# Attention and pair products on one core: six instead of four of a tile's eight score pieces are kept, and x lives in a ring of chunk slots

## The reference, cut to what matters

```
# layer 0, on n = group_norm(x)
f, g, h = Wq n + bq, Wk n + bk, Wv n + bv        # 32, 32 and 256 channels
s       = f^T g                                   # 4096 x 4096 for each batch
beta    = softmax(s, over the first index)
x       = x + gamma * (h @ beta)
# layer 1, on n = group_norm(x)
y       = relu(bn(w1 n + b1))                     # 32 channels
packed  = all 528 products y[i] * y[j]
x       = x + relu(bn(w2 packed + b2))
```

## Time and profile before

| | us |
|---|---|
| median of 3 runs | 2135.08 (2133.08 to 2136.22) |
| the profiled execution | 2135.18 |
| its span | 2133.4 |
| TensorE busy | 2081.3 |
| VectorE busy | 1623.2 |
| ScalarE busy | 1608.0 |
| GpSimd busy | 1321.3 |

### The profile page before, as it was taken

One profiled execution on the slowest core, in us unless ns is written; L12 is line 12 of the kernel. 1 busy time (PEld: TensorE's weight loads), 2 busy tenths in 40 slices (PEclk: granted clock), 3 DMA queues, 4 the chain that ended last, 5 costly groups with the idle time before them and its releaser, 6 DMA issues.

```text
span 2133.4 us, 48577 instructions
## 1 busy us (share of the span) xinstructions
PE 2081.3 (98%) x17838; PEld 1640.4 (77%) x17838; DVE 1623.2 (76%) x3491; ACT 1608.0 (75%) x2582; POOL 1321.3 (62%) x1984
## 2 busy tenths in 40 slices
PE   4899999999999999999999999999999999999999
PEld 2688888888878877877878777777887778777854
DVE  7687877778877777877778887776876767777767
ACT  4577877777777777878777787777877777777767
POOL 3254455556566676776657677676756656566656
PEclk9999999999999999999999999999999999999999
DMA  6054555455467776667378576776635555464622
GB/s 204 21 81 75 75 88 83 84 84 82 81 119 141 138 135 143 135 118 139 71 149 152 117 142 119 142 143 126 130 59 114 117 103 113 97 122 76 118 66 80
DMA packets 592493, 233.63 MB, mean 110 GB/s; under 512 B 541024, under 2 KB 547936, under 8 KB 592224
## 3 DMA queue, kind: packets, MB, share of 16 engines
q1 hardware_dynamic: 592256, 230.53, 56.4%
HBM read 71.83 MB, written 19.92 MB: 43 GB/s over the span
## 4 chain that ended last, share of the span: by engine, by line
PE 92%; DVE 2%; ACT 2%; issue 1%; DMA 1%; SPq 1%; POOL 0%; DVEq 0%; ACTq 0%
PE acc L1763 21%; PE acc L1751 20%; PE acc L1752 20%; PE sps L1576 5%; PE tps L1556 5%; PE acc L1556 5%; PE tps L1627 4%; PE acc L1550 3%; PE tps L1629 2%; PE acc L1627 1%; PE tps L1591 1%; PE tps L1537 1%; PE tps L1613 1%; PE acc L1629 1%; ACT xh L1276 1%
## 5 line engine op out<-in xcount | busy, mean ns | idle before, releaser
L1136 POOL TENSOR_TENSOR kb<-ks,kb 128x512 f16<-128x512 f32 x504 | 599.3, 1194 | 409.6 <-DVE kb L860 235.9
L1314 ACT ACTIVATE ph<-sps,esc 128x512 f16<-128x512 f32 x520 | 356.7, 686 | 345.8 <-PE sps L1576 336.4
L1751 PE MATMUL acc<-hth,ph 128*128 128x257 f16 x2080 | 484.5, 273 | 0.0
L1752 PE MATMUL acc<-htl,ph 128*128 128x256 f16 x2080 | 484.1, 273 | 0.0
L1751 PE MATMUL acc<-hth,kt 128*128 128x257 f16 x2016 | 469.9, 273 | 0.0
L1752 PE MATMUL acc<-htl,kt 128*128 128x256 f16 x2016 | 469.4, 273 | 0.0
L1326 ACT ACTIVATE ks<-ks,kbias,esc 128x512 f32<-128x512 f32 x504 | 407.0, 808 | 0.0
L865 DVE TENSOR_TENSOR pl<-sps,ph 128x512 f16<-128x512 f32 x520 | 355.2, 683 | 48.2 <-ACT sps L1315 46.7
L1315 ACT ACTIVATE sps<-sps,esc 128x512 f32<-128x512 f32 x520 | 340.5, 655 | 0.0
L1763 PE MATMUL acc<-hth,pl 128*128 128x257 f16 x2080 | 318.3, 274 | 0.0
L1763 PE MATMUL acc<-hth,kt 128*128 128x257 f16 x2016 | 308.8, 274 | 0.0
(11 more groups left out here) (253 smaller groups left out, 3606.3 us busy)
## 6 DMA issues: line engine op xcount, KB each, us to landing
rt<-turned SPq DMA_DIRECT2D x96, 256.0 KB, 5.0
xt<-x SPq DMA_DIRECT2D x36, 512.0 KB, 4.3
xb<-x SPq DMA_DIRECT2D x32, 512.0 KB, 5.5
out<-zt SPq DMA_DIRECT2D x45, 256.0 KB, 2.8
kt<-kb SPq DMA_TRANSPOSE x504, 3.2
yb<-turned SPq DMA_DIRECT2D x36, 128.0 KB, 2.8
rt<-turned SPq DMA_DIRECT2D x72, 64.0 KB, 2.3
turned<-yb SPq DMA_DIRECT2D x12, 256.0 KB, 2.1
```

The source lines that it names most:

```text
L1136: tt(kb[:, m % KB_RING, 1], ks[:, m % KS_RING], kb[:, m % KB_RING, 0], ALU.subtract).then_inc(kl_ok, 1)
L1314: A(ph[:, v % SLOTS], sps[v % 2][:], ACT.Exp, scale=esc[:]).then_inc(ph_ok, 1)
L1751: mm(bank[:, 0:C + 1], high[:, q], hth[:, c * QT + q], start=(s8 == 0 and q == 0), stop=False)
L1752: mm(bank[:, 0:C], high[:, q], htl[:, c * QT + q], start=False, stop=False)
```

## The change

Steps 1, 2, 3, 5, 6 and 7 of a tile are kept; only 0 and 4 are scored a second time. The rings get 9, 4 and 5 places, and the kept pieces' work gets positions written out for each of the six. To have room, x becomes a ring of 14 chunk slots (`XR`; before it was 16 chunks), `xn` a single chunk buffer that is handed over by halves, and the order of the value chunks changes. Chunks that are not in the ring when they are needed go through `xt`: 46 passes instead of 36. The statistics of batches 2 and 3 are taken in batch 0 (`LATER_STATS`), each into its own `bx`.

```diff
-KEPT_STEPS = (1, 3, 5, 7)
+KEPT_STEPS = (1, 2, 3, 5, 6, 7)
+EXP_AT = (1, 4, 5, 6, 7, 8)
+CAST_AT = (None, 3, None, 5, 6, 7)
+LOW_AT = (2, 3, 4, 6, 7, 8)
+TURN_AT = (3, 4, 6, 7, 8, 10)
+DIVIDE_AT = 4
+ROW_AT = 6
-KS_RING = 6
-KB_RING = 3
-KT_RING = 4
+KS_RING = 9
+KB_RING = 4
+KT_RING = 5
+XR = 14
-        xb = [sb(f"xb{i}", [P, H2, HW], f32) for i in range(2)]
+        xb = sb("xb", [P, XR, H2, CH], f32)
-        xn = sb("xn", [P, 2, H2, CH], f32)
+        xn = sb("xn", [P, H2, CH], f32)
-        VORD = (6, 0, 1, 2, 3, 4, 5, 7)
+        VORD = (4, 0, 5, 1, 6, 2, 3, 7)
+        def x_slot(b, c):
+            return (b * NCH + c) % XR
+        NEXT_STATS = tuple((J, t) for J, ts in ((0, (8, 11, 15)), (1, (11, 15, 21)), (2, (11, 18))) for t in ts)
+        LATER_STATS = ((3, 2), (3, 13), (3, 20), (4, 2), (4, 9), (4, 17), (4, 25), (5, 2), (5, 9), (6, 18), (6, 21), (6, 25),
+                       (7, 2), (7, 6), (7, 10), (7, 14))
+        def in_place(b, c):
+            return b == 0 or (c < XR - NCH if b == 1 else c < 4)
+        LOAD_AT = [0] + [USED[use] + 2 for use in THROUGH[:-1]]
...
-            for c in range(NCH):
+            for c in range(XR - NCH):
                 load(1, c)
...
-                        if t % NCH in (2, 4, 6) and is_kept_tile(tile + 1):
-                            turn(tile + 1, t % NCH // 2 - 1)
-                        if t % NCH == 1 and is_kept_tile(tile):
-                            turn(tile, KEPT - 1)
+                        while passed < len(THROUGH) and LOAD_AT[passed] <= (b * NCH + J) * NT + t:
+                            pass_through(*THROUGH[passed])
+                            passed += 1
+                        for r in range(KEPT):
+                            if t % NCH == TURN_AT[r] % NCH and is_kept_tile(tile + 1 - TURN_AT[r] // NCH):
+                                turn(tile + 1 - TURN_AT[r] // NCH, r)
...
-                if k >= 2:
-                    dve.wait_ge(xl_ok, k - 1)
-                for h in range(1 if job in SHARED_OUT else H2):
+                for h in range(halves_of(job)):
+                    if k:
+                        dve.wait_ge(xl_ok, H2 * (k - 1) + h + 1)
...
-                        if s8 in (3, 7) and is_kept_tile(tile + 1):
-                            kept_high(tile + 1, s8 // 2)
+                        if s8 in CAST_AT and is_kept_tile(tile + 1):
+                            kept_high(tile + 1, CAST_AT.index(s8))
```

More of the change, by code:

```diff
@@ L100, in build @@
         ot = sb("ot", [P, QT, C], f32)
-        bst = [sb(f"bst{i}", [P, H2, NCH, 6], f32) for i in range(2)]
+        bst = sb("bst", [P, H2, NCH, 6], f32)
+        bx = [sb(f"bx{i}", [P, H2, NCH, 6], f32) for i in range(B)]
         bag = [sb(f"bag{i}", [P, H2, 2], f32) for i in range(2)]
@@ L164, in build @@
         fc_ok, fc_in, xa_ok = sem("fc_ok"), sem("fc_in"), sem("xa_ok")
-        x_in = [[sem(f"x_in{i}_{c}") for c in range(NCH)] for i in range(2)]
+        x_in = [sem(f"x_in{i}") for i in range(XR)]
         xt_in, xt_free = sem("xt_in"), sem("xt_free")
@@ L516, in _ @@
                 spread(c)
+            passed = 0
             for b in range(B):
-                passing = iter([use for use in THROUGH if use[1] == b + 1])
                 for J in range(NCH):
@@ L612, in moments @@
                 carry_wait()
+                found = bst if layer else bx[n]
                 for h in range(H2):
-                    last = V.bn_aggr(bag[layer][:, h], bst[layer][:, h].rearrange("p c k -> p (c k)"))
+                    last = V.bn_aggr(bag[layer][:, h], found[:, h].rearrange("p c k -> p (c k)"))
                 g(last)
@@ L925, in project @@
                 for part in ORDER:
-                    if part[0] == "x" and ("first", 0, part[1]) not in BY_ACT:
+                    if part[0] == "x":
                         normed(("first", 0, part[1]))
@@ L1006, in attend @@
                             qk_low(b + 1, 2 * (J - 3), tps[1])
-                        if b < LASTB and J in STATS:
-                            for i, at in enumerate(STATS[J]):
-                                if t in (at, at + 1):
-                                    next_stats(b + 1, 3 * J + i, t - at)
+                        for h in range(H2):
+                            if b == 0 and (J, t - h) in STATS:
+                                next_stats(*STATS[J, t - h], h)
                         if b < LASTB and J == 2:
@@ L1121, in value_bias @@
                     pool.wait_ge(xh_ok, JOB[made] + 1)
[L1122 to L1123 removed]
+                    pool.wait_ge(xn_ok, XN[made])
                 for h in range(H2):
[L1125 to L1126 removed]
+                    own = xb[:, x_slot(b, J), h]
+                    last = nc.gpsimd.tensor_scalar(own, own, 1.0, gbv[:, h:h + 1], ALU.mult, ALU.add)
                 last.then_inc(bv_ok, 1)
@@ L1184, in _ @@
                             tt(sc[:, K_AA:K_AA + 1], sc[:, K_A2:K_A2 + 1], exps[:, 3:4], ALU.pow).then_inc(set_pool, 1)
-                        if t % NCH == 0 and is_kept_tile(tile - 1):
-                            kept_low(tile - 1, KEPT - 1)
-                        if t % NCH in (1, 3, 5) and is_kept_tile(tile):
-                            kept_low(tile, t % NCH // 2)
+                        for r in range(KEPT):
+                            if t % NCH == LOW_AT[r] % NCH and is_kept_tile(tile - LOW_AT[r] // NCH):
+                                kept_low(tile - LOW_AT[r] // NCH, r)
                         if t % NCH == 7 and tile + 1 < TILES:
@@ L1278, in high @@
                 last.then_inc(xh_ok, 1)
-                if job in BY_ACT:
-                    act.wait_ge(xl_ok, k - 1)
-                    for h in range(H2):
-                        last = A(xn[:, k % 2, h], xb[0][:, h, c * CH:(c + 1) * CH], ACT.Identity,
-                                 bias=nbias[0][:, h:h + 1], scale=rstd[0][:, h:h + 1])
-                    last.then_inc(xa_ok, 1)
             def second_half(job):
@@ L1608, in project_two @@
                 jobs = [("second", n // NCH, n % NCH + e) for e in range(2)]
-                pe.wait_ge(xl_ok, max(JOB[job] for job in jobs) + 1)
+                pe.wait_ge(xl_ok, H2 * (max(JOB[job] for job in jobs) + 1))
                 for i in range(H2):
```

121 lines of the change are left out of this document (62 added, 59 removed).

## The result

The changed kernel takes 2247.19 us (2244.26 to 2252.16, 4 runs) against 2134.08 us of the kernel before on the same chips: a ratio of 1.0532, 95% interval 1.051 to 1.0553. I had forecast 2110, with 2084 to 2146 as the range. The 55 us of score matmuls are gone, and 168 us have come in their place: TensorE's idle time went from 52 to 166 us (span less busy), and the time that it is busy fell by 3 us and not by 55.

A forecast was written before the change was run, and what follows sets the result against it. TensorE, busy 98% of the span, was taken to bound the kernel: 2135.2 - 55.4 (score matmuls) + 14 (kb landings) + 9 (GpSimd in chunk 7) + 7 (early statistics) = 2109.8, said as 2110 us; range 2084 to 2146.

The forecast's parts named there:

- part 2: Waits in the kb ring for late transpose landings at the channel rotations: 0.6 us each, +14 us, bounds 0 to 86.
- The slack of 1.2 steps: Kb ring: piece 4's buffer is free at step 5.0, VectorE's cast comes at about 6.2; landings may take 6.7 us.
- the stall ends with the burst and other chunks have none: Kb-ring stalls stay at the rotations; reason given for taking a sixth of the upper end, 0.6 us each.
- the 24 bursts: Slow transpose landings around channel rotations, 8 a batch in batches 1 to 3, each costing 0 to 3.6 us.
- Part 1: TensorE drops the score matmuls of two more steps a tile: 55.4 us gained; ScalarE and VectorE get lighter.
- Counted at nothing: VectorE's work and casts lengthened beside a fuller GpSimd, up to 239 us on VectorE, add nothing to the time.
- The ks ring: Nine places of the ks ring let GpSimd lag 2 us before VectorE waits for a buffer.
- part 3: GpSimd overloaded in chunk 7 of batches 0 to 2: 3.1 us stall a batch, +9 us, bounds 0 to 20.
- GpSimd's crowd: In chunk 7 of batches 0 to 2 GpSimd has 25.5 us of work in about 18.8 us: +9 us.
- Part 4: x ring and early statistics: VectorE waits for xt loads in batch 0, +7 us, bounds nothing to 17.
- (b): Rival: GpSimd's low parts bound by way of the rings, 0.7 us for each of 96 tiles, 2154 us; chance 0.20.
- the two sentences on the Trainium skill: Shared DMA engines lengthen bursts, 1.2 us a rotation if doubled, sum 2124; port shared by casts and GpSimd makes casts long.

The follow-up runs named there:

- e4: Changed kernel with 13 x chunk slots instead of 14 and six kb buffers instead of four: 2174.3 us.
- e3: Changed kernel with 13 x chunk slots instead of 14, nothing else: 2258.0 us.
- e7: e4 with GpSimd's low part of each kept piece made for only 256 of its 512 columns: 2150.2 us.
- e18: e4 with only the high half of each kept piece transposed, used again in place of the low: 2159.1 us.
- e19: e4 with both GpSimd's low parts and the transposes of kept pieces halved: 2124.8 us.
- e2: Changed kernel with five kb buffers instead of four and eight ks places instead of nine, 14 slots: 2350.9 us.
- e1: Changed kernel with only steps 1, 3, 5, 7 kept and the earlier rings (ks 6, kb 3, kt 4); new x handling stays: 2137.9 us.
- e12: Changed kernel with five kept steps (1, 3, 5, 6, 7), ks 8, kb 5, kt 5, three float16 parts made by ScalarE: 2124.1 us.
- e8: Changed kernel, four kb buffers, with only the high half of each kept piece transposed, used again for the low: 2203.9 us.

## Why the prediction was wrong

**The step that failed** is the first term of part 2, "I take a sixth of the upper end, 0.6 us each: +14 us". Two more buffers were worth 84 us (e4 against e3), where I had priced the ring at 14 and bounded it at 86. I had found the right place, four kb buffers for six pieces, but worked it out for the wrong pieces: piece 4's cast on VectorE, which waited 4 us in the whole run, and piece 2 on ScalarE, 35 us. Piece 0 on ScalarE (466 us) and piece 3's cast (76 us) aren't in the term. By the positions, piece 0 waits for piece 2 of the tile before, whose exps come at step 5 and its own at step 9 of the same count: four steps, 6.4 us. Two exps (1.6), the low part (1.2) and the landing (3.2) fill 6.0 of them, by an estimate from the earlier trace rows, with nothing else in the way; in the quiet tile above the round took 9.0 us (130.72 to 139.76). The slack of 1.2 steps that I gave the ring isn't there.

The reason for the small share failed as well: "the stall ends with the burst and other chunks have none". Batch 0 has no rotation and took 25 us longer, and in batches 1 and 2 the chunks from 3 on took 36 and 38 us longer, while in batch 3, with as many rotations, they took 6. The stalls come mainly with the work for the next batch and not with the 24 bursts alone. That the lateness then goes round from cast to low part, issue, landing and the next cast fits e7, e18 and e19, where two halvings together gave more than their sum; which piece of the next batch's work starts it, no run takes apart.

**Part 1** held in its gain where nothing stalls (0.4 us in 45 tiles) and in its counts: 1072 score matmuls, GpSimd busy 1633.6 us (1620 forecast), ScalarE 120 us less (135). VectorE became 50 us busier where I had 38 less: 504 casts at a mean of 0.641 us cost 323 us, 59 more than at the 0.524 before, and most of the rest is in `xn` (126 us instead of 110) and the second layer's `qh` (27 instead of 16). "Counted at nothing" was wrong for the casts: moving one a tile away gave 12 to 17 us. TensorE's busy time was not 2026 but 2078 us; matmuls at the lower clock last 0.42 us instead of 0.27, and that is a part of it.

**The ks ring** (part 3) I had at 2 us of slack. e2 shows that slack to be real and its end to be steep: one place fewer, 104 us more in spite of a kb buffer more, while four places more brought 3. **GpSimd's crowd** in chunk 7, +9 us, was not told apart by a run. The chunk took some 9 us longer than before in each of batches 0 to 2; with six kb buffers (e4) 10, 4 and 2, so in batches 1 and 2 most of it was the kb ring.

**Part 4** held: 4 us measured (e1) for 7 forecast, all of it in batch 0; VectorE waited 8.0 us for xt by name, before 4.0.

**The rivals.** (b), with 2154 and a chance of 0.20, had the direction. Its mechanism, low parts that make the rings wait, is a part: halving GpSimd's operation gave 24 us, two kb buffers 84. The whole loss of 168 us is 1.3 us for each of 126 tiles where (b) had 0.7 for 96. Nothing in my cases came near 2247, because I let a stall come from one late thing at a time.

Of the two sentences on the Trainium skill, that on all transfers sharing 16 engines ("DMA: Bandwidth & Descriptors", "Issuing engines are not separate DMA queues") would have added 14 us in all, 0.6 at a rotation; the landing's median didn't move (3.2), so these runs don't show it as the cause. That on the shared port ("SBUF — State Buffer", "Who interferes with whom") agrees: the casts' longest went from 1.37 to 1.90 us and their mean rose by 0.12, and with GpSimd's operation at 0.72 us instead of 1.21 the mean fell from 0.704 to 0.552 (e4, e7). By no means all became long: the median stayed at 0.43 in the changed kernel.

## What to carry to other kernels

When more pieces go round through the same buffers, follow one buffer round its whole loop (write, low part, issue, landing, next write) in the order of the engines' programs, and do it in the chunk with the most other work, not in the quiet one; slack that is measured wait by wait is counted several times. Before blaming a wait, compare tile by tile with the kernel before: it shows where the time is lost. Ask of each ring what one place less does: a ring with just enough gives no sign in the profile that the next cut will cost 5% (e2). If the memory gives full rings for five and not for six, take five.

## What the runs showed of the hardware that I had not expected

The granted clock fell after some stalls of 2 us: TensorE idle from 635.5 to 637.5, matmuls at the lower clock from 638.3 to 645.1 us. Not after each: it idled 2.09 us up to 950.4, and the windows around it show the clock at 1.00 (columns as in the earlier trace rows):
```profile
946.00:953.00 7.00, 4.71 (x42) 3.56 (x41) 5.09 (x13) 5.71 (x9) 4.80 (x11) 1.00 0.46 107
953.00:960.00 7.00, 6.03 (x54) 4.76 (x52) 3.88 (x10) 5.00 (x8) 6.28 (x5) 1.00 0.69 124
```
The kernel before, which never paused so long while attending, kept 0.999; the changed one has 0.987, e4 0.994, e12 0.999. e2 lost 217 us with the clock at 0.997, so stalls cost as much without it. No run takes the clock's share apart from the stalls that go with it; 27 us is its upper bound here.

A transpose of half the bytes landed after 2.5 instead of 3.2 us (medians, e8). If the rest grew in proportion, 1.4 of the 3.2 us would go with the size and 1.8 would not; that is an estimate from these two sizes.
